# Order of two transposes in the expert stage of a transformer layer: inner activations first, next tile's rows second

## The reference, cut to what matters

```
gate = x @ W_gate[e]            # 256 -> 512
up   = x @ W_up[e]              # 256 -> 512
h    = silu(gate) * up
y    = h @ W_down[e]            # 512 -> 256
out[token] += weight[token, e] * y      # two experts add to each token
```

## Time and profile before

| what | value |
|---|---|
| median of 3 executions | 2390.77 us (2390.59 to 2395.83) |
| the profiled execution | 2393.78 us, its span 2392.0 us |
| granted TensorE clock over the span | 0.975 |
| PE / DVE / ACT / POOL busy in the span | 95% / 65% / 54% / 36% |
| expert stage, first transpose to last addition's issue | 2016.3 to 2373.0 us |
| tiles in it | 67 |

### The profile page before, as it was taken

How to read it: one execution, slowest core, us unless ns; L and a number is a source line. 1 busy time by engine, 2 the same in 40 slices (tenths; PEclk the granted TensorE clock), 3 DMA queues, 4 the chain that set the end, 5 groups by cost and what they waited for, 6 DMA issues and landing times. The chain is left out here.

```text
span 2392.0 us, 53442 instructions
## 1 busy us (share of the span) xinstructions
PE 2264.0 (95%) x18144; PEld 1987.0 (83%) x18144; DVE 1552.6 (65%) x3393; ACT 1281.5 (54%) x3900; POOL 849.8 (36%) x1008
## 2 busy tenths in 40 slices
PE   5999999999999999999997999999999965999996
PEld 4888888888888888888886899999999953888885
DVE  5656665666566656665655798888989856445442
ACT  4555555555555555555553666666666631445442
POOL 3333333333333323332332122222222231777674
PEclk9999999999999999999998999999999985999998
DMA  5000000000000000000002000000000011444434
GB/s 174 19 10 18 9 18 9 18 17 10 13 14 18 9 18 9 18 9 18 9 1 71 1 13 16 18 9 18 9 18 18 10 45 42 102 80 95 86 52 104
DMA packets 52984, 74.09 MB, mean 31 GB/s; under 512 B 9424, under 2 KB 36816, under 8 KB 52848
## 3 DMA queue, kind: packets, MB, share of 16 engines
q1 hardware_dynamic: 39952, 55.07, 7.2%
q0 software_dynamic: 12960, 18.12, 4.5%
HBM read 55.60 MB, written 21.76 MB: 32 GB/s over the span
## 5 line engine op out<-in xcount | busy, mean ns | idle before, releaser
L356 POOL TENSOR_TENSOR p_sb<-p_sb,rinv 128x512 f32<-128x512 f32 x256 | 283.8, 1108 | 837.1 <-DVE rinv L606 837.1
L528 ACT ACTIVATE p_sb<-s_ps,nmax 128x256 f32<-128x256 f32 x512 | 237.9, 470 | 426.9 <-DVE nmax L587 426.9
L749 POOL TENSOR_TENSOR sp_sb<-sp_sb,srinv 128x512 f32<-128x512 f32 x128 | 133.1, 1040 | 428.4 <-DVE srinv L935 428.4
L58 DVE SCALAR_TENSOR_TENSOR qbd_lo<-m_ps,qbd_hi 64x256 fp32r<-64x256 f32 x256 | 108.1, 422 | 226.7 <-ACT qbd_hi L46 225.0
L57 DVE TENSOR_TENSOR kt_lo<-k_ps,kt_hi 128x512 fp32r<-128x512 f32 x256 | 176.1, 688 | 110.6 <-ACT kt_hi L45 109.0
L45 ACT CAST kt_hi<-k_ps 128x512 fp32r<-128x512 f32 x256 | 151.6, 592 | 130.7 <-PE k_ps L65 130.2
L883 ACT ACTIVATE sp_sb<-sm_sb,snmax 128x128 f32<-128x128 f32 x512 | 199.4, 390 | 7.0 <-DVE snmax L946 3.9
L603 DVE COPY pt_sb<-t_ps 128x512 f32<-128x512 f32 x256 | 176.6, 690 | 38.0 <-PE t_ps L449 34.2
L587 DVE TENSOR_REDUCE nmax<-s_ps 128x2 f32<-128x512 f32 x256 | 174.1, 680 | 0.3 <-PE s_ps L65 0.2
L449 PEld LDWEIGHTS t_ps<-ident,p_sb 128*128 128x128 f32 x1024 | 127.3, 140 | 34.9 <-issue 1.2
L449 PE MATMUL t_ps<-ident,p_sb 128*128 128x128 f32 x1024 | 153.3, 272 | 1.0 <-DVE pt_sb L603 1.0
(11 more groups left out here) (280 smaller groups left out, 7398.6 us busy)
## 6 DMA issues: line engine op xcount, KB each, us to landing
ctx_raw<-in_ctx_t SPq DMA_DIRECT2D x32, 256.0 KB, 2.8
ctx_raw<-in_ctx_t SPq DMA_DIRECT2D x64, 128.0 KB, 2.9
xn<-f_xn SPq DMA_DIRECT2D x16, 256.0 KB, 2.2
acc<-x_sb SPq DMA_DIRECT2D x16, 256.0 KB, 2.3
e_raw<-in_gate SPq DMA_DIRECT2D x8, 512.0 KB, 3.9
e_raw<-in_up SPq DMA_DIRECT2D x8, 512.0 KB, 4.8
e_raw<-in_down SPq DMA_DIRECT2D x8, 512.0 KB, 6.1
x_sb<-in_x SPq DMA_DIRECT2D x1, 3584.0 KB, 15.0
```

The costliest lines, as they stand in the source:

```text
L356: nc.gpsimd.tensor_tensor(prob, prob, inv, ALU.mult).then_inc(norm_done, 1)
L528: ex = nc.scalar.activation(p_sb[:, k, b * J:(b + 1) * J], s_ps[1 - w][:, b * J:(b + 1) * J], ACT.Exp, bias=nmax[:, k, b:b + 1], scale=1.0 ...
L749: nc.gpsimd.tensor_tensor(prob, prob, inv, ALU.mult).then_inc(norm_done, 1)
```

## The change

In PE's step, `turn_h` of the tile before comes first and `turn_x` of the tile to come second. Nothing else is changed: the same instructions, waits, buffers and semaphores, in the other order.

```diff
                 def step(i, before, w, w_before):
 
+                    turn_h(before)
                     turn_x(i + 1)
-                    turn_h(before)
                     gate_up(i, w)
                     down(before, w_before)
```

## The result

Over 22 executions each, the changed kernel takes 2399.61 us (median, 2392.52 to 2404.65) and the kernel before 2394.09 us (2390.24 to 2398.72). The ratio is 1.0024, with a 95% interval of 1.0016 to 1.0031; the medians lie 5.5 us apart. The three executions shown ahead of the prediction (median 2390.77) lay low in that spread. The profiled execution after has a span of 2397.6 us at a granted clock of 0.974, 5.6 us more than the one before.

What follows compares the result with a forecast made beforehand. PE's step (5.18 us) and POOL's scatter round (4.9) were taken as nearly equal, POOL setting the end after the change. 4.1 us gained less 1.1 for holds gave 3.0 off 2390.77, so 2387.8; range 2380 to 2396.

Steps and rivals of the forecast that it cites:

- the 64 rounds: POOL's rounds from third to last scatter: forecast 326.8 us, or 327.9 with holds, against 330.2 before.
- The sign that I had named myself: The prediction is wrong if, among other signs, POOL's `token_out` shows durations of 1 us again and again.
- What PE gains: PE's expert-stage step, without the wait ahead of `turn_x`: 4.92 us, 0.26 less a step, 17 us in all.
- the loop's turn: PE's gap from the last matmul of `down` to the next step: could cost 0.12 to 0.26 us.
- POOL's rounds as the new bound: POOL's scatter rounds stay at 4.9 us and set the end; `token_out` waits rise from 40 towards 60.
- the 0.7 at the start: Ahead of the third scatter, where POOL follows PE: 0.7 us saved.
- After one hit `token_out` comes later than `e_w_lo` in the next step too: DVE's `e_w_lo` holds POOL's `token_out` only once or twice in 18 pieces: 1.1 us lost.
- one hit shifts POOL out of reach: Argument against the slower rival: once held by `e_w_lo`, POOL escapes further holds.
- slower rival: `e_w_lo` holds `token_out` or its scatter's issue in most of 18 pieces: 13.9 us longer, 2404.7; chance 0.12.
- 6 rounds with a load of weights in them, 6.9 each: POOL's scatter rounds that coincide with a weight load: 41.4 us of the 64 rounds.
- That costs nothing at the end, which POOL sets: A later `y_copy`, waiting for `token_out`, holds up PE without adding to the end time.
- The bounds: Limits on the terms: gain from zero to 9.3 us off; cost of holds from 0 to 18 us.

Runs made afterwards that it cites:

- e5: Changed kernel with DVE's `e_w_lo` moved behind `ht_lo` and the weight loads issued in thirds: 2376.56 us, ratio 0.9931 to the kernel before.
- e6: Kernel before (old order) with `e_w_lo` moved behind `ht_lo` and the weight loads issued in thirds: 2392.48 us, ratio 1.0000.
- e11: Changed kernel with three more transposes of `e_xs` per step, slowing PE: 2395.05 us, ratio 1.0009 to the kernel before.
- e3: Changed kernel with DVE's `e_w_lo` moved behind `ht_lo` in the next step: 2386.74 us, ratio 0.9977 to the kernel before.
- e1: Changed kernel with two more transposes of `e_xs` per step, slowing PE: 2394.7 us, ratio 1.0009 to the kernel before.
- e2: Kernel before (old order) with DVE's `move` put ahead of `xt_lo`; PE's step stayed at 5.19: 2396.0 us, ratio 1.0015.
- e9: Kernel before (old order) with `e_w_lo` moved behind `ht_lo`: 2392.37 us, ratio 1.0000.
- e8: e5 with `token_out` in two buffers, written before the wait for the landing, and `y_copy` waiting for `out_gate`: 2370.66 us, ratio 0.9911.
- e4: Changed kernel with each expert's weight load issued in thirds as buffer parts are split: 2381.77 us, ratio 0.9947 to the kernel before.

## Why the prediction was wrong

The forecast was 3.0 us less, 2387.8 us; measured is 5.5 us more than before, at 2399.61, outside the range. Of the 11.8 us between these two times 3.3 are the base, which was 2394.09 in place of 2390.77; the other 8.5 are the change. (That the 64 rounds missed by 11.8 as well is chance.) The change stays under the 0.3% that I had named as measurable, but that is no hit: two terms were wrong by nearly 6 us each, both the same way, and with 22 executions the change is clear of zero. The sign that I had named myself has come, `token_out` at 1 us again and again.

- **What PE gains: right.** The step was to be 4.92 and is 4.87 to 4.88; the loop's turn costs nothing beyond the 0.12. Shown by the table of waits, and priced by e5 against e6 at 16 us, where the prediction had 17. Between the traces of these two the 65 steps differ by 20 us, and POOL's longer tail in e5 takes 3 of it back.
- **POOL's rounds as the new bound: right.** 64 waits for a landing where I said "towards 60", `y_copy` waiting for `token_out`, plain rounds at 4.9, the 0.7 at the start. That it is the pace and not the order is shown by e11.
- **"After one hit `token_out` comes later than `e_w_lo` in the next step too": wrong, the main error.** From the end of a held operation to the next `token_out` is not a whole round but a round less what comes before the issue: 2056.72 to 2060.91 is 4.19 us. `e_w_lo` comes again 4.87 later and lasts 1.2, so the next `token_out` falls into it once more. So "one hit shifts POOL out of reach" was wrong too. I allowed 1.1 for holds; they cost 6.8 in nine rounds, and they are also what ties the load to the scatter, the next error. My slower rival had this mechanism, priced at 18, with 0.12; it did not have the longer load rounds.
- **"6 rounds with a load of weights in them, 6.9 each": wrong size, 5.8 us.** I took the load round of a POOL that is not held. It is no constant but what is left of the load when the scatter is issued, and a hold ties the two starts together. e3 (scatter 2.3 to 2.5 behind the load: 6.24 to 6.68) and the changed kernel (0.44 to 0.50: 7.83 to 8.22) show it from both sides. It is not the whole rule: with the scatter 2.3 to 2.8 behind the load, three of five rounds in e1 and e2 are 7.49, 7.34 and 7.19, the other two 6.52 and 6.66, like e3's 6.24 to 6.68. What makes the three longer is unexplained.
- **"That costs nothing at the end, which POOL sets": right.** The long steps of PE, up to 9.1, are POOL's load rounds passed on.
- **The bounds.** They ran from 9.3 off to 18 on for the holds, and the truth was within them, though the load rounds had no bound of their own. The range ended at 2396 and so left out the worse half of the slower rival, on an argument that I had not followed through for a second round.
- **A reading that changed no term.** I wrote that `token_now` takes 0.19 except beside `e_w_lo`. In the trace before it also takes 0.75 to 0.78 in 20 of 69 cases, nearly all starting 1.1 behind a scatter's issue, which itself lasts 1.6; after, 60 of 69 are so. It hides behind the landing in both.

Open: the round from the 37th to the 38th scatter is 5.8 to 5.9 in nearly all traces, at different times of the step, and the one from 2307.48 in the earlier trace rows is long (5.7 to 6.5) with the old order in every trace but e9's, and in e8 and e11. And why e2 was held at all.

## What to carry to other kernels

Where two loops run beside each other at nearly one rate, a gain on the slower one does not only end at the other. It takes away the slack with which that one absorbed its disturbances, and each comes due in full. So ask not only for the second loop's mean round but for each event that lengthens it, and where in its round these events will fall when it never idles. And when a sound gain doesn't show, look for what it uncovered before it is taken back: here the same edit is worth -0.24% alone and +0.7% behind two edits that do nothing for the old order.

## What the runs showed of the hardware

- A scatter of 128 rows beside a 1.5 MB load lands about when the load does. Issued 0.44 to 2.05 us behind the start of the load, it landed within 0.7 us of the last of the load's three DMAs, in all twelve cases of the traces before and after; alone it lands after 3.8. The next scatter is then issued 8.3 to 9.2 us behind the start of the load in these two and in e3, where the first came 2.3 to 2.5 behind; e1 and e2 have three cases of 9.7 to 10.0, unexplained. The same bytes in thirds, one a round, cost nothing in e4 where the scatter came 1.8 us or more behind (4.76 to 5.13), and up to 0.6 where it came under 1 us behind.
- DVE's `e_w_lo`, which reads two operands from SBUF, also lengthens the issue of an indirect DMA on POOL when that begins after it: 2.56 in place of 1.60 at 2094.31. An issue that began ahead of it kept its 1.60 in all seven cases of the trace before. The Trainium skill, "SBUF — State Buffer", section "Who interferes with whom", has a DVE instruction with two SBUF inputs contend with a GpSimd instruction that reads SBUF, and the order of issue decide who is blocked; the traces agree, by these rows and by `out_gate` at 2055.52 (1.20). But it infers that this kind of DVE operation does not stall the making of descriptors, and the row of 2.56 speaks against leaving an indirect issue out. Such an issue also reads its row numbers from SBUF (`token_out`), and no run here separates that reading from the making of descriptors.
